# A graph layer on one core: the keys' exponentials kept in memory, the edge softmax's shifts made head by head, and a new pace of attention items

## What is computed

```python
x1 = relu(xn @ W_ah + b_ah)
# graph attention, 3 layers of 4 heads, 21250 edges
e = leaky_relu(as_n[src] + ad_n[dst], 0.2)
p = exp(e - segment_max(e, dst)[dst])
out = segment_sum(p / segment_sum(p, dst)[dst] * h[src], dst)
x = x + relu(node_emb @ W_out + b_out) + mix(xn)
# mix: 12 heads of 64, 256 random features
dash = (d ** -0.25) * data @ proj.T
q' = ratio * (exp(dash - diag - max over features) + 1e-4)
k' = ratio * (exp(dash - diag - max over ALL heads, rows, features) + 1e-4)
out = q' (k'.T v) / (q' sum(k'))
# then a switch layer: 8 experts, capacity 195, top-1 routing
```

## Time and profile before

| what | value |
|---|---|
| median of 3 runs | 1723.0 us (1720.8 to 1727.4) |
| the profiled execution | 1728.7 us, its span 1726.9 us |
| PE busy, DVE busy, ACT busy | 1578.6, 1130.7, 681.8 us |
| mean granted clock of PE | 0.96 |

### The profile page before, as it was taken

One profiled execution on the slowest core, in us unless ns is written; L12 is line 12 of the kernel. 1 busy time (PEld: TensorE's weight loads), 2 busy tenths in 40 slices (PEclk: granted clock), 3 DMA queues, 4 the chain that ended last, 5 costly groups with the idle time before them and its releaser, 6 DMA issues.

```text
span 1726.9 us, 24932 instructions
## 1 busy us (share of the span) xinstructions
PE 1578.6 (91%) x9666; PEld 1201.4 (70%) x9731; DVE 1130.7 (65%) x2573; ACT 681.8 (39%) x1359; POOL 410.9 (24%) x251
## 2 busy tenths in 40 slices
PE   3979999999989888999999979999999999986987
PEld 2556666555655566888888879888888966665664
DVE  6678664114466896988989869667875643885223
ACT  3421001122232465767777765434643421441110
POOL 3788888888300000000000000000000000002331
PEclk9989999999999778999999999999999999996999
DMA  9335545454752214222240234344530134645951
GB/s 355 84 57 121 115 78 120 61 92 74 204 177 78 90 53 158 87 79 88 92 136 27 76 126 156 114 145 149 165 124 28 59 113 143 221 179 203 318 152 51
DMA packets 194505, 213.66 MB, mean 124 GB/s; under 512 B 80976, under 2 KB 149214, under 8 KB 194387
## 3 DMA queue, kind: packets, MB, share of 16 engines
q1 hardware_dynamic: 117762, 187.01, 32.7%
q0 software_dynamic: 75760, 22.70, 8.3%
q10 hardware_dynamic: 864, 2.36, 0.4%
HBM read 144.74 MB, written 68.40 MB: 123 GB/s over the span
## 4 chain that ended last, share of the span: by engine, by line
PE 75%; DVE 14%; ACT 4%; issue 3%; DMA 2%; SPq 0%; POOLq 0%; POOL 0%; ACTq 0%; DVEq 0%
PE bank L1047 19%; PE bank L892 13%; PE bank L893 13%; PE bank L891 12%; PE bank L1217 4%; PE bank L1205 3%; PE bank L1073 3%; PE bank L1101 3%; DVE junk L1452 2%; PE bank L1116 1%; PE bank L993 1%; DVE q_max L1521 1%; ACT ef L1921 1%; PE bank L901 1%; DVE eb L1498 1%
## 5 line engine op out<-in xcount | busy, mean ns | idle before, releaser
L1047 PE MATMUL bank<-hb,eb 128*128 128x193 f32 (+3 forms) x2400 | 414.4, 329 | 19.9 <-ACT node L1896 16.1
L1047 PEld LDWEIGHTS bank<-hb,eb 128*128 128x128 f32 (+3 forms) x2400 | 396.4, 189 | 30.9 <-issue 18.5
L2093 POOL DMA_INDIRECT table<-amount,place x170 | 346.2, 2036 | 70.5 <-issue 49.8
L2099 POOL IOTA iota8i<- 128x8 int32 x1 | 0.1, 140 | 942.0 <-DMA node_rows<-node 942.0
L1489 DVE SCALAR_TENSOR_TENSOR eb<-shift_b,as_low,shift_b 128x640 f32<-128x640 f32 (+1 forms) x240 | 196.5, 860 | 9.1 <-DMA shift_b<-shift_rows 9.1
L1882 ACT ACTIVATE eb<-eb,asd 128x640 f32<-128x640 f32 (+1 forms) x240 | 181.5, 813 | 38.1 <-DVE eb L1489 38.1
L1498 DVE SCALAR_TENSOR_TENSOR eb<-eb,count 128x1280 f32<-128x1280 f32 (+1 forms) x120 | 174.5, 1455 | 3.7 <-ACT eb L1882 3.6
L1452 DVE CUSTOM_DVE_ANT_0 junk<-ab,absent 128x1250 bf16<-128x1250 f32 x120 | 174.5, 1454 | 1.6 <-issue 0.2
L891 PE MATMUL bank<-wg_hi,x1T_hi 128*128 128x384 bf16 (+3 forms) x360 | 118.9, 330 | 0.2 <-DVE x1T_lo L1319 0.2
L892 PE MATMUL bank<-wg_lo,x1T_hi 128*128 128x384 bf16 (+3 forms) x360 | 118.8, 330 | 0.0
L893 PE MATMUL bank<-wg_hi,x1T_lo 128*128 128x384 bf16 (+3 forms) x360 | 118.8, 330 | 0.0
(11 more groups left out here) (288 smaller groups left out, 2974.0 us busy)
## 6 DMA issues: line engine op xcount, KB each, us to landing
w<-in_w SPq DMA_DIRECT2D x16, 1152.0 KB, 14.0
shift_b<-shift_rows SPq DMA_DIRECT2D x24, 625.0 KB, 6.0
h_rows<-h_row SPq DMA_DIRECT2D x27, 388.0 KB
hb<-h_rows SPq DMA_DIRECT2D x12, 873.0 KB
ar<-node_rows SPq DMA_DIRECT2D x27, 384.0 KB
table<-zero POOLq DMA_DIRECT2D x3, 3054.0 KB, 19.5
tab<-table SPq DMA_DIRECT2D x27, 312.5 KB, 3.4
qk_rows<-qk_row SPq DMA_DIRECT2D x12, 625.0 KB
```

What stands on the lines that cost most here:

```text
L1047: ins = T.matmul(bank[w // 2][0:M, c0:c0 + GC + 1], p[0:K, u, w * P:w * P + M], hv[0:K, t, 0:GC + 1], start=opens and u == 0 and w % 2 == ...
L2093: G.indirect_dma_start(tables[i], bass.IndirectOffsetOnAxis(place[:, c:c + 1], axis=0), amount16[:, c:c + 1], None, compute_op=ALU.add).th ...
```

## The change

- `k_keep`: when a key tile's product and maximum are there, ACT writes exp(product - the row's own maximum) to `e_out`, and SP stores it (256 KB a tile) in HBM. The bank is only free after that, so `k_top` now waits for `k_kept` instead of `k_max`. A negation `kneg` per tile is added on DVE.
- In the mix a k step has no product and no exponential. `e_load` brings the kept tile back, four steps ahead into a ring of five, and `k_feat` multiplies it with exp(row maximum - diag - global maximum), adds the epsilon, in two operations of 256 columns. The loads of k are gone.
- `shifts` is made for one head instead of four, and `head_in` of the first head stands where the mix begins. Attention items start three steps ahead of the second pair's k steps, before with its last k step; `edge_max` goes on beside them as before.
- The rate of items is 0.33 per mix step and 0.52 after the mix, before 0.5 throughout.
- `warm_mix`: products of bf16 identities (512 columns) into a bank that nobody reads: 18 where the maximum is made, 4 in each k step, 2 in each other step, until the first item is gathered, 124 in all.

```diff
-COUNT_RATE, EARLY_EDGE_RATE, FIRST_EDGE_RATE, EDGE_RATE, ATTENTION_RATE = 0.5, 0.75, 1.1, 0.8, 0.5
+COUNT_RATE, EARLY_EDGE_RATE, FIRST_EDGE_RATE, EDGE_RATE, ATTENTION_RATE = 0.5, 0.75, 1.1, 0.8, (0.33, 0.52)
...
+            yield from (("k_keep", i) for i in unkept)
+            unkept.clear()
...
+    yield "warm_mix", 8
...
+    yield "warm_mix", 4
...
+    yield "warm_mix", 6
...
-    yield from spread(edge_layer(0), lambda: FIRST_EDGE_RATE if "projected" in done else EARLY_EDGE_RATE)
-    while "projected" not in done:
-        yield None
-    yield from paced((attention_steps(done), ATTENTION_RATE), (edge_steps(done), EDGE_RATE))
+    edges = edge_steps(done)
+    yield from spread(edges, lambda: FIRST_EDGE_RATE if "projected" in done else EARLY_EDGE_RATE,
+                      lambda: "projected" in done and "first_shift" in done)
+    yield "head_in", 0
+    yield from spread(edges, lambda: FIRST_EDGE_RATE, lambda: "first_pair" in done)
+    yield from paced((attention_steps(done), lambda: ATTENTION_RATE["mixed" in done]), (edges, EDGE_RATE))
...
+            if lh and t == 0:
+                yield "shift_store", lh - 1
+                done.add("first_shift")
...
-    yield "shifts", l
+        yield "shifts", lh
...
     def features(n):
...
+        if n == 2 * NT:
+            done.add("first_pair")
+        if "open" not in done:
+            yield "warm_mix", 4 if kind == "k" else 2
...
-        if kind:
-            yield "dash", pair, kind, t
+        if n + AHEAD < len(order) and order[n + AHEAD][1] == "k":
+            yield "e_load", NT * order[n + AHEAD][0] + order[n + AHEAD][2]
+        if kind == "q":
+            yield "dash", pair, t
...
             def k_top(i):
...
-                pe.wait_ge("k_max", i - 1)
+                pe.wait_ge("k_kept", i - 1)
...
+            def keep_warm(b, n):
...
+                for _ in range(n):
+                    T.matmul(bank[b][:, :], ident16[:, :], ident16[:, :].unsqueeze(1).broadcast_to([128, 4, 128]),
+                             start=True, stop=True)
...
+                ve.wait_ge("k_max", 2 * i + 1)
+                V.tensor_scalar(kneg[0:R, i:i + 1], kmax[0:R, i:i + 1], -1.0, None, ALU.mult).then_inc(sem["k_max"], 1)
...
+                V.tensor_tensor(ks, ks, kmax[:, :].rearrange("p (a t) -> p t a", t=NT).unsqueeze(3).broadcast_to(
+                    [P, NT, PAIRS, 2]), ALU.add).then_inc(sem["top_v"], 1)
...
             def edge_z(i):
...
-                ve.wait_ge("dash_mm", 2 * NT)
+                ve.wait_ge("dash_mm", NT)
...
+            def k_keep(i):
...
+                se.wait_ge(f"e_out{i % 3}", 16 * (i // 3))
+                se.wait_ge("k_max", 2 * i + 2)
+                A.activation(e_out[i % 3][0:R, :], bank[4 + i % 2][0:R, :], ACT.Exp,
+                             bias=kneg[0:R, i:i + 1]).then_inc(sem["k_kept"], 1)
...
+            def top_spread(_):
+                se.wait_ge("top_v", 5)
+                A.activation(k_shift[:, :, :], k_shift[:, :, :], ACT.Exp).then_inc(sem["k_scale"], 1)
...
+            def k_feat(pair, t):
...
+                se.wait_ge(*kept_in(n))
...
+                    ins = A.activation(e[0:R, hh, :], e[0:R, hh, :], ACT.Relu, bias=eps[0:R, :],
+                                       scale=k_shift[0:R, t, 2 * pair + hh:2 * pair + hh + 1])
...
-            def k_exp(pair, t):
-                exps(pair, "k", t)
...
-                A.activation(e, e, ACT.Relu, bias=eps[0:rows(t), :]).then_inc(sem["k_feat"], 1)
...
-            def shifts(l):
-                sy.wait_ge("shift_turned", l + 1)
+            def shift_store(lh):
+                sy.wait_ge("shift_turned", lh + 1)
...
+            def k_keep(i):
...
+                sy.wait_ge("k_kept", i + 1)
+                S.dma_start(e_rows[pair, at(t), :], e_out[i % 3][0:rows(t), :]).then_inc(sem[f"e_out{i % 3}"], 16)
...
+            def e_load(n):
+                sy.wait_ge("qk_mm", NC * 2 * PAIRS)
+                if n >= AHEAD + RING:
+                    sy.wait_ge("feat_used", used(n - RING, "k"))
+                load_kept(n)
...
             def pair_in(pair):
...
+                if pair == 0:
+                    for n in range(AHEAD):
+                        load_kept(n)
...
-                S.dma_start(keys_of(pair)[:, :, :], qk_rows[1, pair]).then_inc(sem[f"k_in{i}"], 16)
```

More of the change, by code:

```diff
@@ L140, in paced, with spread @@
         yield None
-def spread(steps, rate):
+def spread(steps, rate, enough):
     due = 0.0
-    while True:
+    while not enough():
         due += rate()
@@ L293, in edge_layer @@
             yield "edge_max", NT * lh + t
+            if lh and t == 0:
+                yield "shift_store", lh - 1
+                done.add("first_shift")
             yield None
-    yield "shifts", l
+        yield "shifts", lh
     yield None
-def edge_steps(done):
-    for l in range(1, LAYERS):
-        yield from edge_layer(l)
+    yield "shift_store", LH - 1
     done.add("edges")
@@ L315, in of_half, with opened @@
         return stage
+    def opened(i):
+        done.add("open")
+        return []
     def mark(i):
@@ L653, in program @@
         cursor[0] = r_b
-        kT = [put(f"kT{i}", [128, 2, N], BF16) for i in range(2)]
+        ek = [put(f"ek{i}", [P, 2, FEATS]) for i in range(RING)]
         qT = [put(f"qT{i}", [128, 2, N], BF16) for i in range(2)]
@@ L669, in program @@
         cursor[0] = r_c
-        k_first, q_first = put("k_first", [128, 2, N], BF16), put("q_first", [128, 2, N], BF16)
+        e_first = [put(f"e_first{i}", [P, 2, FEATS]) for i in range(AHEAD)]
+        q_first = put("q_first", [128, 2, N], BF16)
         v_first = put("v_first", [P, NT, 2, HD + 1])
@@ L745, in program @@
         cursor[0] = r_e
+        e_out = [put(f"e_out{i}", [P, 2 * FEATS]) for i in range(3)]
+        assert cursor[0] <= r_f - size([P, N], U16)
+        cursor[0] = r_e
         hb = [put("hb0", [P, NT, HW]), hb1]
@@ L869, in row_bank, with kept_of, kept_in, used @@
             return 5 + (i % 3 if i < 2 * NT * LAYERS else i % 2)
-        def keys_of(pair):
-            return kT[pair % 2] if pair else k_first
+        def kept_of(n):
+            return e_first[n] if n < AHEAD else ek[(n - AHEAD) % RING]
+        def kept_in(n):
+            i = n - AHEAD
+            return ("e_first_in", 16 * AHEAD) if i < 0 else (f"e_in{i % RING}", 16 * (i // RING + 1))
+        def used(n, kind):
+            return dash_of(n // NT, kind, n % NT) + 1
         def queries_of(pair):
@@ L1010, in top_turn @@
                 pe.wait_ge("top_v", 1)
+                pe.wait_ge("k_kept", PAIRS * NT)
                 T.transpose(bank[5][0:1, 0:P], top[0:P, 0:1], identP).then_inc(sem["top_pe"], 1)
@@ L1079, in q_turn @@
                 R = rows(t)
-                g = dash_of(pair, "q", t)
                 q = NT * pair + t
-                pe.wait_ge("mix_exp", g + 1)
+                pe.wait_ge("mix_exp", q + 1)
                 pe.wait_ge("q_feat", q - 1)
@@ L1221, in tensor_program @@
             mine = dict(keys_turn=keys_turn, turn=turn, x1=x1, h=h, as_rows=as_rows_, v=v, qk=qk, norms=norms, k_top=k_top, top_turn=top_turn, top_spread=top_spread,
-                        count_turn=count_turn, gather=gather, dash=dash, k_sum=k_sum, q_turn=q_turn, q_out=q_out,
+                        count_turn=count_turn, warm_mix=warm_mix, warm_last=warm_last, gather=gather, dash=dash, k_sum=k_sum, q_turn=q_turn, q_out=q_out,
                         row_turn=row_turn, row_mm=row_mm, f_turn=f_turn, logits=logits,
@@ new lines, in q_exp @@
+            def q_exp(pair, t):
+                R = rows(t)
+                q = NT * pair + t
+                se.wait_ge("top_v", 5)
+                se.wait_ge("q_max", 2 * q + 2)
+                if q >= 4:
+                    se.wait_ge("feat_used", used(q - 4, "q"))
+                for hh in range(2):
+                    ins = A.activation(ef[q % 4][0:R, hh, :], bank[3 + q % 2][0:R, hh * FEATS:(hh + 1) * FEATS],
+                                       ACT.Exp, bias=q_shift[0:R, t, hh:hh + 1])
+                ins.then_inc(sem["mix_exp"], 1)
```

162 lines of the change are left out of this document (83 added, 79 removed), and 4 rows, old and new, of the table TAKEN_OVER.

## The result

The kernel after is slower: 1742.8 us (median of 4 runs, 1739.6 to 1746.3) against 1725.2 us of before in the same session, 17.6 us more. The ratio of the runs is 1.0115, 95% interval 1.0085 to 1.0146, some 20 us. The forecast was 1710 us; the result lies 0.8 us above the range's upper end, on the other side of "no change". The profiled execution took 1744.6 us.

The account below looks back on a forecast made before the run. PE, busy 91%, bounds the kernel before; DVE was to become the mix's bound. Terms -59.6 - 16 + 52.3 + 9 + 1 = -13.3 us, from 1723.0 to 1709.7, rounded 1710 us; range 1684 to 1742.

Parts of the forecast that it names:

- The rate of 0.52 there changes their places, not PE's sum: Behind the mix: the later item rate only moves where items stand and leaves PE's total work unchanged; priced at nothing.
- PE has no idle time to give: Beside the output products: PE has no idle time, so the 16 items moved there cost their full 3.27 us each.
- The paid-back items: Behind the mix: 16 attention items gathered later than before, at 3.27 us each, +52.3 us.
- The four later pairs: Mix, last four pairs: DVE becomes the bound, 62.5 us a pair for 77.4; -59.6 us, between -74.8 and -48.4.
- the 94% I named: Sign of being right: a later pair of 61 to 64 us with DVE busy 94% or more and PE at 85%.
- The first two pairs: Start of the mix: 125.0 us become 109; -16 us, between -22 and 0.
- It rests on the clock: First two pairs: the -16 us depends on unread products lifting the half clock; 0 if the clock is no better.
- could cost 3 us once: Mix start: kept tiles 5 to 8 stand behind the first head's rows on SP, possibly 3 us once; loads priced at nothing.
- The projection: Key products wait longer for banks held until the exponential: +9 us, between 0 and 25; +1 us at its end.
- The clock's falls (20%): Rival, 20%, ends slower: with DVE as bound PE idles more, and the clock falls repeatedly in the mix's k stretches.
- Late kept tiles (8%): Rival, 8%, mix: kept tiles come late and a k step is 0.3 us longer for 50 steps, 1725 us.
- The projection (12%): Rival, 12%: the projection does not hide the exponentials; 1 us in each of 30 groups, 30 instead of 9, 1731 us.

## Why the prediction was wrong

The terms by stage miss by +10.6 (projection), +13.9 (mix) and +4.7 us (behind the mix), 29 us in all, all in one direction.

**"The rate of 0.52 there changes their places, not PE's sum"** is the step that failed worst, not by its size but because it was priced at nothing and had no range. PE's work indeed hardly changed. But PE has idle time behind the mix when a late load reaches it through ACT and DVE, and the places decide that; and beside the mix rows, where PE is the bound, 10.3 us of half clock came with such waits and cost time too, some 5 us by the estimate above. Shown: 9.3 us by undoing it in the kernel after, 6 to 10 us by doing it alone in the kernel before. What I read as "PE has no idle time to give" was true of the stretch I looked at, 1240 to 1383, and not of the ones before it: PE waited 8.7 us in one piece between the mix and the mix rows.

**The paid-back items: right.** 15 items moved (300 products), not 16. With the late rate at 0.5 the three last stages grew by 551.6 - 498.4 - 5.8 + 0.1 = 47.5 us for 15 x 3.27 = 49.

**The four later pairs: nearly right.** From q start to q start they take 62.5 us each, to a tenth the forecast's number, but that cut is not the forecast's, and the tenth is luck. By its own cut they take 63.4 us (253.7 / 4) after 76.8, so -53.4 us for -59.6, inside its ends. DVE is busy 91% (227.8 of 249.9), not the 94% I named, and PE as much (227.3). Both stand near full, and neither is the sole bound.

**The first two pairs: half of it wrong**, -16 forecast, -8.2 measured. "It rests on the clock", and the clock hardly sets that stretch. Two pairs of runs show it: before without and with unread products, 82.0 and 82.0 us at 0.72 and 0.98; after with and without, 80.8 and 81.0 at 0.93 and 0.64; up to the third pair's first `k_sum` the better clock is worth 2 to 3 us in both. One part of the miss is the first k stretch: from `top` to the first q step's products it takes 28.9 us. In it PE waits 5.6 us for a kept tile, issued at 607.0, which took 8.6 us to land, where I had "could cost 3 us once". With these loads on GpSimd's queue it takes 20.1, about the forecast's 19.5 and 1; but only 3.3 of these 8.8 us are left at the third pair. What holds the stretches behind it was not settled.

**The projection: undersized**, +10 taken with its end, +20.6 measured, inside its ends of 0 and 25, and about midway between my 10 and the rival's 30. I had 0.9 us per late wait for the exponential; PE's waits for it came as eight of up to 4.4 us, and, as I read ACT's order, because the exponential stands there behind `sq`, the count's copies (1.25 us each) and a weight's split. That order was not tried otherwise; shown are the 10 to 14 us, by the two runs that free the bank. The clock has a part in the 20.6 us that I had at nothing: some 22 us of 440 to `top` ran at half clock, against 11 in before (an estimate from the stages' means, 0.93 and 0.96, and the levels 1.00 and 0.50). (The three hand-overs that I put at 0.2 us are 38, 34 and 54 ns from end to start in before's trace, 0.13 in all; in after's, with the negation ahead of the exponential, they are 38, 94 and 55 ns, 0.19.) The row that I should have used is ACT's order, not a sum of durations.

**The rivals.** The clock's falls (20%): two of them, just inside the range's end of 1742 us, would give almost the measured time, by luck. No run shows the price of one fall. The rival's place was the mix's k stretches, and there falls are short, with 0.93 to 0.95 in the mix's windows, and a quarter of the clock more or less (0.64 and 0.93, 0.72 and 0.98) was worth 0 to 3 us. Where PE is the bound, its work got longer with the falls: beside the mix rows 20 products took 5.21 us for 3.43, and in the projection the 11 us more at half clock are some 5 us of work, an estimate. Neither the forecast nor the rival had a fall in these places. Before showed one already, which I overlooked behind the mix: 0.50 from 1029.5 to 1039.7, around the wait of 8.7 us. Late kept tiles (8%) are real, 36 us of ACT's waits, and worth 2 us of the end. The projection (12%) was the nearest in kind. None named the later rate.

**Sum.** With the bank wait, SP's place for the loads and the late rate taken out, the time is 1718.0 us; the forecast was 1710. So the change's idea gives something, 5 to 6 us of the 13.3 by the medians and ratio; the rest of the way to 1742.8 is mostly the bank's longer hold in the projection and the late load behind the mix, each with half clock beside it (some 22 us in the projection, 10.3 beside the mix rows).

## What to carry to other kernels

Where a program is interleaved by rates, any change of a rate shifts every boundary (end of a head, first row, reload of weights) against every queue behind it: look there for loads that come to stand behind another track's store and rows, and put 10 us of either sign on the change instead of nothing. Before paying for a clock, compare the engine's busy time with the stretch, and see whether it would be shorter: here 72.0 busy of 82.0 us at 0.72 became 76.3 of 82.0 at 0.98, with the unread products in it. Where the engine is the bound, look for low clock behind its long waits: here 10.3 us of it came behind waits of 2.3 and 5.5 us. When a value that was thrown away is kept, count who holds its buffer now, and what stands ahead of that holder on its own engine.

## What the runs showed of the hardware

- In one stretch a lower clock cost nothing. Where the mix of the kernel after begins, with PE busy 63.81 of 81.0 us at a mean granted clock of 0.64 without the unread products, and 70.74 of 80.8 at 0.93 with them, the stretch took the same time within 0.2 us.
- Beside the mix rows, where PE was busy 178.57 of 187.7 us, it did cost. There waits of 2.3 and 5.5 us came with 10.3 us at 0.50 to 0.51 (20 products of a gather in 5.21 us against 3.43), some 5 us of the stage, an estimate (half of 10.3).
- 512-column products of bf16 identities (18 in the gap, 2 or 4 a step) brought the granted clock of that stretch from 0.72 to 0.98 in the kernel before, at 82.0 us with and without them, and a ratio of 0.9988 for the whole.
- In this kernel the multiplication of a kept tile, read from SBUF, with a per-row factor and an added per-row term took ACT 599 ns for 256 columns, against 473 for the exponential of as many, read from a bank, with one per-row term (1.27 times):

```profile
L1995 ACT ACTIVATE ef<-bank,q_shift 128x256 f32<-128x256 f32 (+1 forms) x120 | 50.4, 473 | 65.5 <-DVE q_shift L1580 65.4
L1983 ACT ACTIVATE ek<-ek,eps,k_shift 128x256 f32<-128x256 f32 (+1 forms) x112 | 58.6, 599 | 36.0 <-DMA ek<-e_rows 36.0
```

- A 256 KB load that took 3.5 us from issue to landing as a median took 8.1 to 8.6 us for the four issued from 607.0 to 609.2, between a head's and a pair's rows, all in the kernel after.
